# Graph attention on one core: the ring of gathered rows from two turns to three, with the skip rows and projection weights kept in DRAM

## The reference, cut to what matters

```python
def _tconv(x, src, dst, ea, Wq, bq, Wk, bk, Wv, bv, We, Ws, bs):
    q = (x @ Wq + bq).reshape(n, H, C)
    k = (x @ Wk + bk).reshape(n, H, C)
    v = (x @ Wv + bv).reshape(n, H, C)
    e = (ea @ We).reshape(-1, H, C)
    alpha = jnp.einsum('ehc,ehc->eh', q[dst], k[src] + e) / jnp.sqrt(jnp.float32(C))
    amax = jax.ops.segment_max(alpha, dst, num_segments=n)
    ex = jnp.exp(alpha - amax[dst])
    w = ex / (jax.ops.segment_sum(ex, dst, num_segments=n)[dst] + 1e-16)
    out = jax.ops.segment_sum((v[src] + e) * w[:, :, None], dst, num_segments=n)
    return out.reshape(n, D) + x @ Ws + bs
```

## Time and profile before

| | us |
|---|---|
| median of three runs (3180.64 to 3187.31) | 3185.88 |
| span of the profiled execution | 3640.5 |
| TensorE busy, profiled | 2313.1 (64%) |
| GpSimd busy, profiled | 2015.5 (55%) |
| VectorE busy, profiled | 1974.9 (54%) |
| ScalarE busy, profiled | 1172.0 (32%) |

### The profile page before, as it was taken

How to read it: one execution, slowest core, us unless ns; L and a number is a source line. 1 busy time by engine, 2 the same in 40 slices (tenths; PEclk the granted TensorE clock), 3 DMA queues, 4 the chain that set the end, 5 groups by cost and what they waited for, 6 DMA issues and landing times. The chain is left out here.

```text
span 3640.5 us, 67503 instructions
## 1 busy us (share of the span) xinstructions
PE 2313.1 (64%) x14712; PEld 1806.8 (50%) x14713; DVE 1974.9 (54%) x5388; ACT 1172.0 (32%) x3723; POOL 2015.5 (55%) x2306
## 2 busy tenths in 40 slices
PE   5567999726666666666666681666566666666660
PEld 3335999515455455545555441455454555454550
DVE  5554222326556556656566652566566665565666
ACT  1001555303333333333333430233333333333343
POOL 3500222346666666666666267466666666666637
PEclk6656999856656666556565665565666656666665
DMA  7787111223333333333335113233333333333342
GB/s 206 213 262 213 37 37 37 77 79 108 110 111 108 103 104 110 110 109 111 103 107 94 26 46 117 79 110 111 109 111 109 100 109 111 109 111 104 104 44 71
DMA packets 276049, 384.84 MB, mean 106 GB/s; under 512 B 121804, under 2 KB 207772, under 8 KB 275676
## 3 DMA queue, kind: packets, MB, share of 16 engines
q0 software_dynamic: 80768, 220.05, 21.6%
q1 hardware_dynamic: 145628, 163.04, 14.2%
q10 hardware_dynamic: 49536, 0.55, 0.8%
HBM read 360.42 MB, written 23.02 MB: 105 GB/s over the span
## 5 line engine op out<-in xcount | busy, mean ns | idle before, releaser
L1351 POOL DMA_INDIRECT wide<-kv,a_source x1664 | 1691.0, 1016 | 922.7 <-issue 470.9
L1385 PE MATMUL psum<-wide,a_hot 128*128 128x136 f32 x3328 | 855.4, 416 | 391.5 <-issue 215.7
L1374 PE MATMUL psum<-wide,a_hot_t 128*128 x4992 | 697.9, 287 | 511.3 <-issue 333.4
L1579 DVE TENSOR_TENSOR acc<-acc,psum 128x136 f32 x1664 | 488.8, 294 | 914.5 <-remote 681.8
L1385 PEld LDWEIGHTS psum<-wide,a_hot 128*128 128x128 f32 x3328 | 695.8, 292 | 513.1 <-issue 317.3
L1374 PEld LDWEIGHTS psum<-wide,a_hot_t 128*128 128x128 bf16 x4992 | 516.3, 115 | 678.6 <-issue 591.7
L1441 ACT ACTIVATE a_edge_q<-psum 128x16 f32<-128x16 f32 x416 | 74.6, 180 | 1770.8 <-remote 1379.9
L1449 ACT ACTIVATE a_hot<-iota_n,a_spot 128x128 f32<-128x128 f32 x1664 | 526.5, 390 | 25.3 <-PE psum L1385 12.6
L1498 DVE TENSOR_TENSOR a_product<-psum,wide 128x512 f32<-128x512 f32 x416 | 284.6, 684 | 178.1 <-remote 85.0
L1453 ACT ACTIVATE a_hot<-a_hot,ones 128x512 f32<-128x512 f32 x416 | 300.2, 722 | 13.6
L1501 DVE TENSOR_REDUCE a_score<-a_product 128x16 f32<-128x512 f32 x416 | 286.4, 688 | 14.4
(11 more groups left out here) (263 smaller groups left out, 2257.5 us busy)
## 6 DMA issues: line engine op xcount, KB each, us to landing
acc<-in_edge_attr SPq DMA_DIRECT2D x344, 192.0 KB, 3.5
a_place<-places SPq DMA_DIRECT2D x104, 512.0 KB
wide<-kv,a_source POOLq DMA_INDIRECT x1664
kv<-acc SPq DMA_DIRECT2D x49, 128.0 KB
kv<-p_pairs SPq DMA_DIRECT2D x49, 128.0 KB
c_node<-drec ACTq DMA_DIRECT2D x344, 1.5 KB
a_cut<-breaks SPq DMA_DIRECT2D x208, 8.1 KB
acc<-in_x SPq DMA_DIRECT2D x49, 64.0 KB
```

Of the source, the lines that this page charges most:

```text
L1351: pool.indirect_dma_start(out=ring[:, at.b, n, :], out_offset=None, in_=kv[:, :], in_offset=bass.IndirectOffsetOnAxis(ap=source[at.b][:, n ...
L1374: last = pe.matmul(query_out(q)[:, t, :], hot_t[:, b, q * QUAD + t, :], rows, start=(s == 0), stop=(s == SPLIT - 1), skip_group_check=True)
L1385: last = pe.matmul(sum_out(q, t), hot[q % 2][:, t, :], ring[:, (at.b + back) % 2, q * QUAD + t, LEAD:KV], start=True, stop=True, skip_grou ...
L1579: dve.tensor_tensor(here, here, sum_out(q, t), ALU.add).then_inc(added, 1)
```

## The change

The ring holds three turns (`TURNS = 3`), 24 quads, so a gather waits for the sums of the quad 24 earlier. It takes the SBUF space of `skip` and of three tables of weights (`wall[1]`, `ball[1]`, `ball_again`), which now lie in the ring's third part. The skip rows are stored to DRAM as they are made (update and project stage), and both are read back by SyncE at the end of `attend_stage`, when turn 23, the last that uses the third part, has been summed. `source`, `edge_w` and `spot` have three buffers, `source` is loaded two turns ahead. `cut` comes by one DMA of 128 rows from a new table `cuts` in DRAM, which the collect stage copies from `breaks` by four DMAs. The hardware loop's body is six turns (`ROUND`), the least that both ring and pairs of buffers divide: two turns ahead of it, three rounds, then eight written out and two to drain. TensorE's loop body goes from 511 rows of program to 1525.

```diff
+TURNS = 3
+ROUND, OPENING = 2 * TURNS, 2
+    cuts = nc.dram_tensor("cuts", [TCAP // G, P, P + 1], BF16).ap()
+    skips = [nc.dram_tensor(f"skips{n}", [P, ROWS], F32).ap() for n in (1, 2)]
+    shaped_1 = nc.dram_tensor("shaped_1", [P, 2 * ALL], F32).ap()
...
-        wide = sb("wide", [P, RING + 2 * G * KV])
+        wide = sb("wide", [P, RING + TURNS * G * KV])
+        LENT = RING + (TURNS - 1) * G * KV
-        skip = sb("skip", [P, ROWS])
+        skip = wide[:, LENT:LENT + ROWS]
+        lent = [wide[:, LENT + ROWS + n * ALL:LENT + ROWS + (n + 1) * ALL] for n in range(3)]
...
@@ store_lists, collect stage
+                for g in (0, 1):
+                    sp.wait_ge(codes_out[g], 32 * ((CH + 1 - g) // 2))
+                by_turn = m["breaks"].rearrange("(g t) e -> g t e", t=G)
+                for h in range(HEADS):
+                    sp.dma_start(m["cuts"][:, h * G:(h + 1) * G, :], by_turn).then_inc(lists_out, 16)
...
@@ update_stage, SyncE's store (project_stage alike)
+                sp.wait_ge(emitted, PROJECT_STEPS * w + 3)
+                sp.dma_start(m["skips"][0][:, bass.ds(w * P, P)], m["skip"][:, bass.ds(w * P, P)]).then_inc(skips_out, 16)
+            sp.dma_start(m["shaped_1"][:, 0:ALL], m["wall"][1]).then_inc(shaped_out, 16)
+            sp.dma_start(m["shaped_1"][:, ALL:2 * ALL], m["ball"][1][:, :]).then_inc(shaped_out, 16)
...
@@ turns_of
-    for g in (0, 1):
+    for g in range(OPENING):
         step(Turn(eng, g))
-    with eng.Fori(1, (NG - 2) // 2) as r:
-        for d in (0, 1):
+    with eng.Fori(1, (NG - OPENING) // ROUND) as r:
+        for d in range(OPENING - ROUND, OPENING):
             step(Turn(eng, d, r))
-    for g in range(NG - 2, NG + 2):
+    for g in range(NG - ROUND, NG + 2):
         step(Turn(eng, g))
...
@@ attend_stage
-    RING = 2 * QUADS
+    RING = TURNS * QUADS
...
             def load_cuts(g, b):
-                for h in range(HEADS):
-                    sp.dma_start(cut[b][h * G:(h + 1) * G, :], breaks[bass.ds(g * G, G), :]).then_inc(cut_in[b], 16)
+                sp.dma_start(cut[b][:, :], cuts[bass.ds(g, 1), :, :].rearrange("a p e -> p (a e)")).then_inc(cut_in[b], 16)
...
+                if at.has(-2):
+                    at.wait(multiplied, QUADS, 0)
+                    load_source(g + 2, (at.d + 2) % TURNS)
                 if at.has(-1):
-                    at.wait(made_hot, 2, 2)
-                    load_places(g + 1, 1)
-                    at.wait(multiplied, QUADS, 0)
-                    load_source(g + 1, other)
                     at.wait(linked, LINKS, SUNK - LINKS)
                     load_cuts(g + 1, other)
-                    at.wait(linked, LINKS, SHARED - LINKS)
-                    load_weight(g + 1, other)
-                if at.has():
                     at.wait(hot_there, QUADS, -QUADS)
-                    load_spots(g, at.b)
+                    load_weight(g + 1, (at.d + 1) % TURNS)
+                    load_spots(g + 1, (at.d + 1) % TURNS)
                 if at.has(-2):
                     at.wait(made_hot, 2, 3)
                     load_places(g + 2, 0)
+                    at.wait(made_hot, 2, 4)
+                    load_places(g + 2, 1)
...
+            last_there = NG - 1 - (NG - TURNS) % TURNS
+            sp.wait_ge(products, QUADS * last_there + QUADS - 1 + SUM + 2)
+            sp.dma_start(m["skip"], m["skips"][layer]).then_inc(refilled, 16)
...
-                    if at.has(2):
+                    if at.has(TURNS):
                         at.wait(products, QUADS, q - RING + SUM + 2)
```

More of the change, by code:

```diff
@@ L132, in build @@
         ahead_in, loaded = sem("ahead_in"), sem("loaded")
+        wall = [lent[0], lent[1]]
+        ball = [lent[2], ahead.enter_context(nc.sbuf_tensor("ball1", [P, ALL], F32))]
+        ball_again = lent[0]
         w1a = ahead.enter_context(nc.sbuf_tensor("w1a", [FEAT, HID], F32))
@@ L951, in _ @@
                 sp.wait_ge(pairs_out[k], 16 * ((NW + 1 - k) // 2))
+            sp.wait_ge(skips_out, 16 * NW)
+            sp.wait_ge(shaped_out, 16 * 2)
         @block.tensor
@@ L1172, in __init__ @@
         self.eng, self.d, self.r, self.known = eng, d, r, {}
-        self.b = d % 2
-        self.now = d if r is None else r * 2 + d
+        self.b, self.third = d % 2, d % TURNS
+        self.now = d if r is None else r * ROUND + d
     def has(self, back=0):
@@ L1191, in wait, with wait_buffer @@
             self.eng.wait_ge(sem, self.count(per, c))
-    def wait_pair(self, sem, per, back=0):
-        half = per // 2
-        self.wait(sem, half, per - half * back - half * ((self.d - back) % 2))
+    def wait_buffer(self, sem, depth, per, back=0):
+        loads = per * ((self.d - back) // depth + 1)
+        if self.r is not None:
+            loads = self.eng.snap(self.r * (ROUND // depth * per) + loads)
+        self.eng.wait_ge(sem, loads)
 def turns_of(eng, step):
-    for g in (0, 1):
+    for g in range(OPENING):
         step(Turn(eng, g))
-    with eng.Fori(1, (NG - 2) // 2) as r:
-        for d in (0, 1):
+    with eng.Fori(1, (NG - OPENING) // ROUND) as r:
+        for d in range(OPENING - ROUND, OPENING):
             step(Turn(eng, d, r))
-    for g in range(NG - 2, NG + 2):
+    for g in range(NG - ROUND, NG + 2):
         step(Turn(eng, g))
@@ L1222, in attend_stage @@
         "bank", "psum", "ident", "iota_n", "ones", "low", "lane", "q3", "ring", "acc"))
-    kv, trec, places, breaks, links = m["kv"][layer], m["trec"], m["places"], m["breaks"], m["chain"]
+    kv, trec, places, cuts, links = m["kv"][layer], m["trec"], m["places"], m["cuts"], m["chain"]
     WIDTH = G + 1
     WEIGH, SUM, ADD = (QUADS + n for n in (4, 5, 6))
-    RING = 2 * QUADS
+    RING = TURNS * QUADS
     SUMMED, ENDED, ENTERED, SUNK, SHARED, LINKS = 2, 4, 10, 13, 14, 16
@@ L1337, in _ @@
             load_places(1, 0)
+            sp.wait_ge(made_hot, 2)
+            load_places(1, 1)
             turns_of(sp, step)
+            last_there = NG - 1 - (NG - TURNS) % TURNS
+            sp.wait_ge(products, QUADS * last_there + QUADS - 1 + SUM + 2)
+            sp.dma_start(m["skip"], m["skips"][layer]).then_inc(refilled, 16)
+            if layer == 0:
+                sp.dma_start(m["wall"][1], m["shaped_1"][:, 0:ALL]).then_inc(refilled, 16)
+                sp.dma_start(m["ball_again"], m["shaped_1"][:, ALL:2 * ALL]).then_inc(refilled, 16)
+            sp.wait_ge(refilled, 16 * (3 if layer == 0 else 1))
         @block.gpsimd
@@ L1351, in step @@
                         pool.indirect_dma_start(
-                            out=ring[:, at.b, n, :], out_offset=None, in_=kv[:, :],
-                            in_offset=bass.IndirectOffsetOnAxis(ap=source[at.b][:, n:n + 1], axis=0)
+                            out=ring[:, at.third, n, :], out_offset=None, in_=kv[:, :],
+                            in_offset=bass.IndirectOffsetOnAxis(ap=source[at.third][:, n:n + 1], axis=0)
                             ).then_inc(rows_in[at.b][q], 16)
@@ L1384, in sums @@
                         at.wait(added, G, (q - 1) * QUAD + 1 - G * back)
-                    last = pe.matmul(sum_out(q, t), hot[q % 2][:, t, :], ring[:, (at.b + back) % 2, q * QUAD + t, LEAD:KV],
+                    last = pe.matmul(sum_out(q, t), hot[q % 2][:, t, :], ring[:, (at.d - back) % TURNS, q * QUAD + t, LEAD:KV],
                                      start=True, stop=True, skip_group_check=True)
@@ L1461, in enter_columns, with grow @@
                 act.activation(decay[:, :], drop_out, ACT.Exp, scale=begins[:, 0:1]).then_inc(decayed, 1)
-            def grow(at, b):
-                act.activation(ring[:, b, :, LEAD:LEAD + HEADS], grown_out.rearrange("p (h t) -> p t h", h=HEADS), ACT.Exp
+            def grow(at):
+                act.activation(ring[:, (at.d - 1) % TURNS, :, LEAD:LEAD + HEADS], grown_out.rearrange("p (h t) -> p t h", h=HEADS), ACT.Exp
                                ).then_inc(grown, 1)
@@ L1553, in weigh @@
             def weigh(at, back, q):
-                here = ring[:, (at.b + back) % 2, q * QUAD:(q + 1) * QUAD, :]
+                here = ring[:, (at.d - back) % TURNS, q * QUAD:(q + 1) * QUAD, :]
                 values = here[:, :, FEAT:KV].rearrange("p t (h c) -> p t h c", h=HEADS)
```

53 lines of the change are left out of this document (31 added, 22 removed).

## The result

| kernel | median of its runs, us | range | runs |
|---|---|---|---|
| before, measured beside it | 3185.31 | 3180.64 to 3187.31 | 4 |
| changed | 3209.91 | 3205.19 to 3214.05 | 4 |

The changed kernel takes 1.0079 times as long, 95% interval 1.0067 to 1.0091: slower by 24.6 us. The forecast was 3189 us with "no change" as the likeliest case (3180 to 3196), in a range of 3115 to 3220. Two of all the timed executions lie far off and are left out of the ratios: one of the kernel before took 3758.64 us (beside experiments 5 to 8) and one of experiment 4 took 6780.07 us; neither left a trace.

A forecast was written before the change was run, and what follows sets the result against it. The prediction took GpSimd's nearly unbroken gathers to pace plain attention stages, blaming TensorE's lateness mostly on the profiled execution. Its terms, 0 + 0 + 2 + 1 = +3 us, gave 3189 us, range 3115 to 3220.

The forecast's parts named there:

- no change: Whole kernel: plain time stays within the cost terms, 3180 to 3196 us; chance 46%.
- The pace: Attention stages, plain run: GpSimd gathers nearly without pause, 32 x (1.016 + 0.283) = 41.6 us a turn.
- The ring, 0: Attention stages: the longer lead removes no waits in plain runs, 0 us; at most the two openings, 73.3 us.
- Indices, breaks, cuts: 0 + 0 + 2: Earlier index load 0, one DMA of breaks instead of four 0, cuts table in collect stage 2 us (0 to 12).
- The stores, +1: Update and projection stages: skip-row stores covered by SyncE's slack, about 1 us from last stores; uncovered, 20 us.
- The read-back: Each attention stage's end: 3.7 MB take 34 us within 47 us, hidden, 0; not over 10 if gathers slow it.
- The loop of six, 0: Attention stages: fewer back-branches but more fetched code, taken as 0 us.
- Rival 2: Attention stages: longer code arrives late, up to +44 us (3232), half 3210; 22% with uncovered store or cuts, late code 14.
- the signs that the prediction named: For a rise over 10 us: instruction packets, idle "issue" time before gathers, update stage's length against 340 us.
- Rival 1: Attention stages: waits remain in plain runs and the longer lead removes them, 3113 to 3180 us; 32% with rival 3.
- 3198.6: Whole kernel: profiled span 3640.5 us less GpSimd's 441.9 us of slot waits, 13 us above the plain median.
- The profiled span: Whole kernel, profiled: little change or a fall, 3640 us less 0 to 100, since TensorE sets the pace there.

The follow-up runs named there:

- 5: Kernel before with a loop body of six turns on TensorE alone: 3190.67 us, ratio 1.0018.
- 6: Kernel before with a loop body of six turns on VectorE, ScalarE, GpSimd and SyncE, TensorE's staying at two: 3189.99 us, ratio 1.0014.
- 7: Kernel before with skip rows also stored to DRAM and read back over themselves once turn 23 is summed; weights not read back: 3199.63 us, ratio 1.0038.
- 8: Kernel before with the padding edges' source indices spread over the nodes instead of all 0: 3166.38 us, ratio 0.9933.
- experiment 4: Changed kernel with three turns of ring, but gathers waiting for the sums of the quad 16 earlier, as with two turns: 3213.88 us, ratio 1.0083.
- experiment 1: Kernel before, unchanged, profiled a second time ("the second profile" of before): one run, 3179.18 us.
- experiment 2: Kernel before with only the loop body of six turns, on all engines: 3198.69 us, ratio 1.0037.
- 3: Changed kernel with the read-back held until a layer's last gathers have landed and been used: 3203.98 us, ratio 1.0057.
- 9: Changed kernel with the padding edges' source indices spread over the nodes: 3187.68 us, ratio 1.0012 against the kernel before.
- 10: Kernel before with the padding's source indices spread, run again on the same chip as the changed kernel with it: 3165.28 us, ratio 0.9935.

## Where the prediction was right and where it was wrong, point by point

The 3209.91 us lie inside the stated range of 3115 to 3220, but by its width: they are 21 us above the forecast, outside the likeliest case's own 3180 to 3196. The argument on the ring held. The loss comes from terms that the sum had at nothing or too small: the loop of six, the read-back, the cuts table and the stores.

**The pace** (right, in part by luck). "In a plain run GpSimd gathers nearly without a pause: a turn is 41.6 us" was inferred from two totals; the second profile of before has 41.1 us and no waits. The two terms were both off, and against each other: a gather takes 0.982 us, not 1.016, and the pause before it is 0.305 us (473.4 / 1552), not 0.283, which was the idle time of "issue" shared among all gathers, those too that had waited.

**The ring, 0** (right). The changed kernel with its longer lead taken away is as slow (experiment 4).

**Indices, breaks, cuts: 0 + 0 + 2** (cuts too small). No experiment took them alone, but the traces show the cuts. SyncE's timeline in the collect stage, in the second profile of before:

```profile
182.10 9.07 SPq L371 DMA_DIRECT2D chain<-skip  x9
192.53 17.70 SPq L356 DMA_DIRECT2D acc<-in_edge_attr  x26
```

and in the changed kernel:

```profile
182.15 9.20 SPq L379 DMA_DIRECT2D chain<-wide  x9
191.46 3.21 SPq L389 DMA_DIRECT2D cuts<-breaks  x4
196.03 13.88 SPq L364 DMA_DIRECT2D acc<-in_edge_attr  x21
```

From the first `chain` store to the next load of edge rows it takes 10.4 us before and 13.9 with the change. The other profiles agree: 9.9 to 10.5 us in the seven without the cuts (the unusual first profile of before left out), 13.3 to 13.9 in the four with them. The buffers don't cover it: the remaining 176 loads take 125 to 127 us in all eleven, and the update stage's first load follows at 323.6 to 328.5 us without the cuts and at 328.5 to 334.2 with them. So the cuts cost 3 to 4 us, inside the 0 to 12 that the prediction gave. The times of experiments 2 and 7 leave 0.04% of the 0.79%, about 1 us, which their intervals of 4 us and more to either side don't tell from 3.5. The load of the indices for the first turns of both layers shows as 6 to 7 us in both kernels.

**The stores, +1** (too small). The step "a delay of 0.4 us fits into 1.5" holds in the main: 49 stores at 0.43 us would be 21 us if nothing covered them, and the stage grew by some 3, the projection stage by nothing that shows. So +3 or so.

**The read-back, "Hidden; 0, and not over 10 if the gathers slow it"** (this step failed). The time it has is 47 us and I took it to need about 34 (it took 20.0), so I called it hidden. But the question was not whether it ends in time; it was who stands beside it. Its packets share the DMA engines with the last gathers, for whose rows VectorE waits, and these are on the path that sets the layer's end. The bound of 10 I gave for the wrong reason, as a delay of the read-back by the gathers. It delays them, by some 4 us a layer, 8 to 9 in all (experiments 3, 7 and 9).

**The loop of six, 0** (this step failed). It costs 0.37%, 12 us. The argument was that layer two, in which small engines fetch code, has "also x582" gathers in as many us, "so a small engine that refetches costs nothing". In that profile GpSimd was held up by TensorE, which hides a few ns a gather. And in the second profile of before layer two's gathers do take 5.5 us longer than layer one's (1073.4 against 1067.9); in the other three profiles with the loop of two on all engines (7, 8, 10) it is 4 to 6 us. With the loop of six the small engines fetch in layer one as well: q14 has 6 packets from 800 to 1700 us in experiment 1 and 53 in experiment 2, and 55 and 52 from 2050 to 2950 us. In the mean of five profiles with the loop of six against these four, layer one's gathers take 7 us longer (1077.8, 1070.8) and layer two's 3 (1078.8, 1075.9). That agrees with a price on the small engines' fetching, but single executions differ by as much, and experiments 5 and 6 don't split the cost so. A cost of half a per cent can't be excluded from rows of a stretch in which another wait sets the pace.

**Rival 2, the longer code** (half right). 12 us lies near the low end of what it foresaw, and its sign is right. Its mechanism isn't: GpSimd's idle time before the gathers did not grow (512.6 us against 513.2), and the code did not "arrive late" for it; the gathers last longer. That its "half of it: 3210" is the measured total is luck, since the loop makes only half of the loss. Of the signs that the prediction named for a loss of over 10 us, the packets and the update stage's length moved, and the idle time before gathers did not. The Trainium skill, Runtime: NRT & Kernel Launch, Instruction fetch mechanics, has a taken branch out of the kept blocks stall for a fetch. The packets do show that more code is fetched (q8 from 30 to 117, q14 from 87 to 131), but no row shows the stall before the gathers of GpSimd, which sets the pace. **What stays open** is how more fetched code makes a gather 6 ns longer. It could be the fetches' traffic, or another timing of the other engines' work beside the gather; no run here tells these apart, and the pages of experiments 5 and 6 differ by less than executions do.

**Rival 1, waits remain** (wrong). There were none. The shorter gather that I weighed for it is there (982 ns, not 1016: 1691.0 - 1634.3 = 57 us less), but no waits fill its place: more than half of it is taken back by issue, since a gather that had waited has no pause counted (idle time without the waits 922.7 - 441.9 = 480.8, and 513.2 now, 32 us more). The net, 24 us, is about the 21.2 by which 3198.6 stood above the second profile's 3177.4.

**The profiled span, "3640 less 0 to 100"** (wrong). It fell by 435.2 to 3205.3, as the stammer of TensorE belongs to one execution and not to profiles as such. The prediction put it down to profiling, and so expected it again.

The sum by what was measured: ring 0, loop 12, stores 3, read-back 8 to 9, cuts 3 to 4: 26 to 28, against 24.6, with an interval of about 4 us to either side on the total and on the loop's part.

## What to carry to other kernels

Before a buffer is made deeper, compare the profile's span with the timed runs: a wait that only the profiled execution has is worth nothing, and a second profile of the same kernel settles it in one run. A transfer that "fits" into the last stretch is not hidden if it shares the DMA engines with loads on which that stretch waits; start it after the last of them, even if it then ends later (here it landed some 7 us later, and still 30 us before the last sums). And look at what padding does: taking away the gathers of one and the same row gave 21 us here, nearly as much as the whole change cost.

## What the runs showed of the hardware that was not expected

- Gathers whose 128 indices are all one row: DMA engines 94% busy at 80 GB/s, and 12.1 us to land at most; with indices spread, 35% busy at 102 GB/s in the same stretch of layer one, and 3.1 us to land at most; both times of landing are layer two's. By packets (engines' time over packets), 16 x 30 x 0.931 / 862 = 0.52 us a packet against 16 x 30 x 0.347 / 1104 = 0.15 us.
- One execution of the same program on one core was 15% longer than another (3640.5 against 3177.4 us), with the same gathers and the same work, TensorE's matmuls trickling and GpSimd waiting for them. It was seen in one profile of twelve. Whether the 3758.64 and 6780.07 us of two executions without a trace were the like is not shown.
- A read-back of 3136 KB took 20.0 us from issue to landing beside the last gathers and 9.8 us after them; the slowest gather beside it landed after 17.8 us instead of 12.1.
- A loop body of six turns instead of two costs 0.37%, with GpSimd, which sets the pace, not seen waiting for code before its gathers (512.6 us of idle time against 513.2), in two parts (TensorE's loop, the others' loops) that add up.
